# The gate's product of a one-core AdaLN block: tokens standing instead of moving

## The reference

```python
mod = (silu(c) @ wmod)                      # shifts, scales and gates of two halves
h = layernorm(x) * (1 + ca) + sa            # x: 4096 tokens x 256 channels
x = x + ga * linear_attention(h)            # 16 heads of 16, two key/value sets
h = layernorm(x) * (1 + cb) + sb
scores = sigmoid(h @ gate_w + bias)         # gate_w: 256 x 8
top_scores, top_idx = top_k(scores, 2)      # then normalised to weights w
routed = sum over the 2 experts of w * 0.1 * (gelu(h @ up_w + up_b) @ down_w + down_b)
shared = (gelu(h @ sw_up + sb_up) @ sw_down + sb_down) * 0.1
out = shared + routed;  out = out / (max |out| + 1e-6)
x = x + gb * out
```

## Time and profile before

| | |
|---|---|
| median of 3 runs | 975.01 us (974.97 to 976.18) |
| profiled execution, its own time | 978.68 us |
| its span | 976.9 us |
| mean granted clock of TensorE | 0.94 of full |
| TensorE busy in the span | 864.6 us (89%), 5989 products |
| weight loads busy | 793.8 us (81%) |
| VectorE, ScalarE, GpSimd busy | 648.4, 474.5, 415.6 us (66%, 49%, 43%) |

### The profile page before, as it was taken

The page is one execution under the profiler, slowest core; times in us unless marked ns, Lnnn a source line. Parts: engine busy times, 40 slices in busy tenths (PEclk is TensorE's granted clock), DMA queues, the critical chain, the costliest instruction groups (busy, mean ns, idle before and its releaser), DMA issues. The chain is left out here.

```text
span 976.9 us, 21511 instructions
## 1 busy us (share of the span) xinstructions
PE 864.6 (89%) x5989; PEld 793.8 (81%) x5990; DVE 648.4 (66%) x1737; ACT 474.5 (49%) x879; POOL 415.6 (43%) x407
## 2 busy tenths in 40 slices
PE   6899998469999999999873999998999999999982
PEld 5687887458788787787773999998999999999982
DVE  5688775466886786877673676665666666666652
ACT  3665553114544543444442765555556655555530
POOL 3724500211522514414330066655666566666564
PEclk9999999659999998999995999999999999999996
DMA  8120000500210202202248133333333333344442
GB/s 280 56 87 1 1 1 0 172 0 2 89 67 24 90 7 84 89 0 89 80 150 286 52 100 93 92 113 114 87 89 90 90 88 82 78 87 88 100 81 40
DMA packets 64384, 78.58 MB, mean 80 GB/s; under 512 B 23089, under 2 KB 52746, under 8 KB 64176
## 3 DMA queue, kind: packets, MB, share of 16 engines
q0 software_dynamic: 21568, 35.20, 14.5%
q1 hardware_dynamic: 41392, 41.12, 13.5%
q10 hardware_dynamic: 1344, 1.31, 0.4%
HBM read 45.44 MB, written 41.55 MB: 89 GB/s over the span
## 5 line engine op out<-in xcount | busy, mean ns | idle before, releaser
L1668 PE MATMUL psUp<-eT,wup 128*128 128x256 f32 x1632 | 204.8, 286 | 11.4 <-issue 5.7
L1668 PEld LDWEIGHTS psUp<-eT,wup 128*128 128x128 f32 x1632 | 198.5, 192 | 16.5 <-issue 14.3
L1690 PE MATMUL psE<-wdn,gTh 128*128 128x256 f32 x1088 | 199.3, 286 | 0.0
L1690 PEld LDWEIGHTS psE<-wdn,gTh 128*128 128x128 f32 x1088 | 169.8, 193 | 0.0
L1690 PE MATMUL psE<-wdn,gTl 128*128 128x256 f32 x544 | 154.1, 283 | 0.0
L1925 POOL DMA_INDIRECT out<-fin,oidx x68 | 109.3, 1608 | 23.1 <-issue 15.9
L1729 ACT ACTIVATE gu<-psUp,ubias 128x256 f32<-128x256 f32 x272 | 113.4, 468 | 9.9 <-PE psUp L1668 5.0
L1793 DVE TENSOR_TENSOR gTl<-gu,gTh 128x512 fp32r<-128x512 f32 x136 | 93.8, 689 | 32.9 <-ACT gTh L1734 31.4
L1036 PE MATMUL psU<-h2T,su 128*128 128x512 f32 x384 | 109.3, 423 | 4.6 <-ACT gf L1118 4.6
L1748 ACT ACTIVATE ys<-yc,meta 128x256 f32<-128x256 f32 x68 | 30.9, 502 | 165.7 <-DVE yc L1813 165.7
L1906 POOL DMA_INDIRECT gx<-shared_part,meta x68 | 69.4, 1020 | 94.7 <-DMA shared_part<-ys,widx 74.2
(11 more groups left out here) (264 smaller groups left out, 1484.5 us busy)
## 6 DMA issues: line engine op xcount, KB each, us to landing
hin<-expert_in SPq DMA_DIRECT2D x36, 256.0 KB
X<-in_L_attn_x SPq DMA_DIRECT2D x8, 512.0 KB, 7.6
shared_part<-prow SPq DMA_DIRECT2D x8, 512.0 KB, 6.0
out<-X SPq DMA_DIRECT2D x8, 512.0 KB, 4.4
shared_part<-sh SPq DMA_DIRECT2D x7, 512.0 KB, 3.3
raw_up<-in_L_ffn_up_w SPq DMA_DIRECT2D x3, 1024.0 KB, 5.5
raw_dn<-in_L_ffn_down_w SPq DMA_DIRECT2D x3, 1024.0 KB, 9.2
expert_in<-prow SPq DMA_DIRECT2D x8, 272.0 KB, 7.4
```

The costliest lines, as they stand in the source:

```text
L1668: mm = nc.tensor.matmul(psU[:, c, (m % 2) * TR:(m % 2 + 1) * TR], wup[s][:, a, k, m * P:(m + 1) * P], eT[:, u, b, k], start=(n == 0), stop ...
L1690: mm = nc.tensor.matmul(psE[:, u, h * C:(h + 1) * C], (gTh, gTl)[a][:, u, m, h * P:(h + 1) * P], wdn[s][:, b, m], start=(n == 0), stop=(n ...
```

## The change

The gate's product swaps its operands. For each of the four tiles of 128 tokens, the transposed tokens stand (128x128) and 8 weight columns move: 4 x 6 = 24 products instead of 6. The logits come out by token, 128 x 32 in the bank `psZ[0]`, so the copy to `lgT` (`gate_copy`), the four transposes (`turn_gate`), their two semaphores and TensorE's waits for them are left out. `gate_read` takes its input from `psZ`. The gate no longer waits for the last gelu of the stage before, as it does not write `psU`. Since `turn_z(0)` writes the same bank later, it waits for `gate_read` (`gt_ev`). Nothing is changed in the DMAs or on GpSimd and ScalarE.

```diff
--- before.py
+++ after.py
@@ -818,7 +818,6 @@
     rs2 = b2("rs2", [P, 2, 2, TG], F32)
     zT = b2("zT", [P, 2, CK, HALF], F32R)
     z2 = b2("z2", [P, TG, C], F32)
-    lgT = z2[0:E, 0:HALF // C].rearrange("e a c -> e (a c)")
     h2 = b2("h2", [P, 2, TG, ROW], F32)
     h2T = b2("h2T", [P, 2, 2, CK, HALF], F32R)
     gf = b2("gf", [P, 2, HALF], F32)
@@ -904,10 +903,10 @@
 
     names = ("q_pre", "nm_mm", "nm_ev", "rq_ok", "o_mm", "o_ev", "stat2", "self2", "rse2",
              "rstd2", "zo_ok", "tz_mm", "tz_hi", "tz_lo", "xb_ok", "a_mm", "x_ev", "z2_ok", "h2_set", "h2_ok",
-             "th_mm", "th_hi", "th_lo", "gt_row", "gt_cp", "gt_mm", "gt_ev", "gt_sc", "rt_dve", "rt_oh", "rt_mm", "pos_ok",
+             "th_mm", "th_hi", "th_lo", "gt_mm", "gt_ev", "gt_sc", "rt_dve", "rt_oh", "rt_mm", "pos_ok",
              "scat", "u_mm", "u_g", "u_hi", "u_lo", "d_mm", "sh_ev", "sh_st", "x_st", "zero_st")
     (q_pre, nm_mm, nm_ev, rq_ok, o_mm, o_ev, stat2, self2, rse2, rstd2, zo_ok, tz_mm, tz_hi,
-     tz_lo, xb_ok, a_mm, x_ev, z2_ok, h2_set, h2_ok, th_mm, th_hi, th_lo, gt_row, gt_cp, gt_mm, gt_ev, gt_sc, rt_dve, rt_oh,
+     tz_lo, xb_ok, a_mm, x_ev, z2_ok, h2_set, h2_ok, th_mm, th_hi, th_lo, gt_mm, gt_ev, gt_sc, rt_dve, rt_oh,
      rt_mm, pos_ok, scat, u_mm, u_g, u_hi, u_lo, d_mm, sh_ev, sh_st, x_st, zero_st) = [sem(n) for n in names]
 
     def staggered(eng, body):
@@ -929,7 +928,7 @@
         psZ = mem.enter_context(nc.psum_tensor("psZ", [P, 2, HALF], F32))
         psO = mem.enter_context(nc.psum_tensor("psO", [P, HALF], F32))
         psM = mem.enter_context(nc.psum_tensor("psM", [P, HALF], F32))
-        NORM, GATE, RANK, TOTAL = 0, 64, 96, 128
+        NORM, RANK, TOTAL = 0, 96, 128
 
         @block.tensor
         def _(pe):
@@ -960,6 +959,8 @@
 
                 def turn_z(k):
                     pe.wait_ge(zo_ok, TG * g + TG)
+                    if ffn_on and not k:
+                        pe.wait_ge(gt_ev, f + 1)
                     if later(g, 1):
                         pe.wait_ge(th_lo, 2 * g - 1 + k)
                     for t in range(TG):
@@ -991,23 +992,13 @@
                 def gate():
 
                     pe.wait_ge(th_lo, 2 * f + 2)
-                    if later(f, 1):
-                        pe.wait_ge(u_g, MK * f)
-                    n = 0
-                    for k in range(CK):
-                        for a, b in PASSES:
-                            mm = nc.tensor.matmul(psU[0:E, 1], gw[:, b, k], h2T[:, r, a, k],
-                                                  start=(n == 0), stop=(n == 5))
-                            n += 1
-                    mm.then_inc(gt_row, 1)
-
-                def turn_gate():
-                    wait(pe, gt_cp, f + 1)
-                    if att_on:
-                        wait(pe, nm_ev, g + 1)
                     for t in range(TG):
-                        mm = nc.tensor.transpose(psM[:, GATE + t * E:GATE + (t + 1) * E],
-                                                 lgT[:, t * P:(t + 1) * P], ident[0:E, 0:E])
+                        n = 0
+                        for k in range(CK):
+                            for a, b in PASSES:
+                                mm = nc.tensor.matmul(psZ[:, 0, t * E:(t + 1) * E], h2T[:, r, a, k, t * P:(t + 1) * P],
+                                                      gw[:, b, k], start=(n == 0), stop=(n == 5))
+                                n += 1
                     mm.then_inc(gt_mm, 1)
 
                 def rank():
@@ -1064,8 +1055,6 @@
                 chunk(0)
                 if att_on:
                     outs(0)
-                if ffn_on:
-                    turn_gate()
                 chunk(1)
                 if att_on:
                     outs(1)
@@ -1254,14 +1243,9 @@
                     ins.then_inc(rt_dve, 1)
                     wait(dve, rt_dve, ROUTE * f + n[0])
 
-                def gate_copy():
-                    dve.wait_ge(gt_row, f + 1)
-                    dve.wait_ge(h2_ok, TG * f + TG)
-                    nc.vector.tensor_copy(lgT, psU[0:E, 1]).then_inc(gt_cp, 1)
-
                 def gate_read():
                     dve.wait_ge(gt_mm, f + 1)
-                    nc.vector.tensor_tensor(lg[:], psM[:, GATE:GATE + TG * E].rearrange("p (t e) -> p t e", e=E),
+                    nc.vector.tensor_tensor(lg[:], psZ[:, 0, 0:TG * E].rearrange("p (t e) -> p t e", e=E),
                                             gb_row[:].unsqueeze(1).broadcast_to([P, TG, E]), ALU.add
                                             ).then_inc(gt_ev, 1)
 
@@ -1326,8 +1310,6 @@
                 if att_on:
                     norm_read()
                     norm_inverse()
-                if ffn_on:
-                    gate_copy()
                 if att_on:
                     out_read(0)
                 if ffn_on:
```

## The result

The change makes the kernel slower: 1001.4 us median (995.5 to 1002.8, 4 runs) against 975.6 before (975.0 to 978.7, 4 runs), a ratio of 1.023 (95% interval 1.020 to 1.026). The medians are 25.8 us apart; by the ratio it is 22. The forecast was 990 with a range of 977 to 997: right direction, too small by 11 us, outside the range. The profiled executions, 978.7 and 1002.1 us, are 23.4 apart where the forecast had 15, so some 3 of the 11 us are the spread between executions and 8 are the forecast's.

What follows compares the result with a forecast made beforehand. Each stage was taken as bound by gate start to `up(2)`, 8.83 us, lengthened by thin products and lost clock. Short spells +12.1, long +17.7, middle +15 on 975.0 gave 990.0 us, range 977 to 997.

Steps and rivals of the forecast that it cites:

- The chain and the place: Gate start to `up(2)`: gate, `up(0)`, `outs(0)`, attention read, logits read, sigmoid, gelu(0); 8.83 us before, its delay delays the stage.
- The pace of a small product: New gate's 24 products take the norms' pace: 0.116 us each at full clock (2.78 us), 0.214 at half (5.13).
- The full-clock sum of 9.30 us per stage: Gate start to `up(2)` without any clock effect: 9.30 us against 8.83, +0.5.
- The direction of the clock: TensorE's clock was expected to fall to half in nearly every stage, in or right after the gate.
- The place of the fall: The clock falls on average half-way through the gate: 12 products at full clock, 12 at half.
- Rows 4 (long): Stage at half clock through norms, gate and all of `up(0)`; the long spell in seven later stages gives +17.7 us.
- rows 6 (short): Clock falls near 367.7 and is back at 371.1, 3.4 us; the short spell sums to +12.1 us.
- So a stretch of thin products is enough to lose the clock: Norms plus gate, thin for 3.3 to 3.9 us before, 4.7 to 5.3 after, lose the clock without a real pause.
- The clock as before: Rival: the clock falls only where it fell before; +4.4 us, 979.4 us, chance 0.11.
- the swallowed loss: Rival: gapless gate products count as work, no fall is left; +0.7 us, 975.7 us, chance 0.08.
- the faster one: Rival: standing loads run ahead, gate product under 0.096 us, `outs(0)` ends earlier; about -7, 968 us, chance 0.06.

Runs made afterwards that it cites:

- the best version: Kernel before, wide gate kept, its logits in the other bank, copy, turns and logits read moved later, sigmoid behind gelu(1): 966.3 us, 0.987.
- the kernel with filler: Kernel after with 12 dense products of 512 columns added per stage, result unread, ahead of the gate's wait and between its thin products: 1013.9 us, 1.038.

## Why the prediction was wrong in size

**Right.** The chain and the place: all of the loss lies between the gate's start and `up(2)`, and the rest of each stage passes it on unchanged. The pace of a small product, from the row of the norms, 0.116 us at full and 0.214 at half clock. The last gate, all thin products at full clock, took 2.70 us, 0.113 each; the first, all at half, 5.12, 0.213 each. The two kinds of instruction in after:

```profile
L999 PEld LDWEIGHTS psZ<-gw,h2T x192: 186/216/338, 213.8 to 503.9; 128*128 128x128 f32 x192
L999 PE MATMUL psZ<-gw,h2T x192: 252/281/356, 213.8 to 504.0; 128*128 128x8 f32 x192
```

Their own durations (0.19 to 0.34 for a load, 0.25 to 0.36 for a product) say little; the pace is in the starts. The 81 ns of the Trainium skill (TensorE: Matmul & The Clock Gate, Back-to-back issue gap) for such a pair were not seen in this kernel with f32 loads. The full-clock sum of 9.30 us per stage was met by the stages that kept it: 9.44 with 128 columns, 9.56 with 256 of which 0.2 is the longer stream. The direction of the clock was right: each of the eight stages had half clock. The place of the fall was right on average too: in the stages 2 to 7 the clock fell 6, 16, 12, 4, 19 and 16 products into the gate, 12 in the mean, which is the half-way that the forecast took.

**Wrong.** The step that failed is the length of the spell: "Rows 4 (long) and rows 6 (short) both exist, so I take the middle". Short gave +12.1 us, long +17.7; measured +22.7 between gate and `up(2)`. Between gate and `up(2)`, each of the stages 2 to 7 had 6.8 us of half clock or more, none a single spell of 3.4. The stage at 254.91 was forecast at 10.9 or 11.7 us and took 12.6: there the clock fell after 6 of the 24 products and not after 12, so the gate took 4.57 us where I had 3.96, and `up(0)` 2.70 for 2.56. In the five stages behind it `outs(0)` was at half clock as well, 1.56 us to the start of `up(1)` where 0.8 to 0.9 is usual, and I had put it at full. Leaving out the fifth stage, that is 0.3 to 1.0 us per stage beyond the long case. The fifth, which had two spells before and for which I had +0.1 (short) or +0.9 (long), got 10.2 us of half clock and +2.7. The first gate cost +3.3 in place of +2.6, again by `outs(0)` and `up(1)` at half. The last was +1.3 as forecast, but that was luck: the forecast had the spell inside the gate, and in the trace the whole gate ran at full clock (2.70 us for 1.40), the clock fell 0.7 us into `up(0)`, and gate end to `up(2)` took 4.4 us as before, as the turns (0.34) and the wait of 0.95 were gone.

Behind it stands a reason that was wrong: "So a stretch of thin products is enough to lose the clock" was right, but I counted the old gate into that stretch, "whose products use 8 columns of the array". The two kernels with twelve added products speak against it: behind 6 products with 8 standing and 512 moving columns the twelve kept the clock in six of seven later stages of the trace, ahead of them they lost it in all seven. That rests on one trace of each, and four of ten executions of the first kernel were as slow as the second. By that reading the thin stretch of before was the norms alone, 1.85 us, and the change made it 4.6, two and a half times as long and not 40% longer. In the trace the rest of it then ran at half clock, which stretched it (the gate took 3.2 to 4.8 us in stages 2 to 7), and the clock was back only in `outs(0)` or `up(1)`, behind 2.7 us of `up(0)`. That the spell is 6.8 us and not 3.4 because the block is so long is argued, not shown: the same block behind `outs(0)` still had one spell of 6.8 among shorter ones.

**The rivals.** The clock as before (979.4) and the swallowed loss (975.7) are out by the clock column; the faster one (968) by the pace. Its "about -7" does not come out of the terms given for it (-4.8, the lost falls of 3.7 and 1.2 for the first gate are -9.7), which changes nothing here. The rule of the Trainium skill quoted there (TensorE: Matmul & The Clock Gate, Why this matters for your kernels), to keep TensorE continuously busy, is not enough in this trace: the thin gate follows the norms without idle time at 254.91 and the clock is gone before it ends.

**How the loss divides.** With 256 moving columns the same number of products and loads gave 987.1: about 14 of the 22 to 26 us go with the clock, and the other 8 to 12 are the added work (1.3 us per stage, less 0.3 for the turns), with what the remaining spells add. Half clock between norms and `up(2)` grew by 30.5 us; as work at half clock takes twice its time, that is an estimated 15 us, which fits. It is not a strict split, as that kernel has 0.2 us more work per stage and its own chance of spells.

## What to carry to other kernels

Swapping the operands so that the big one stands turns 6 long streams into 24 weight loads with almost nothing behind them; the price is not only the loads' pace (24 x 0.113 against 6 x 0.235 us) but the clock of everything around. If such thin products are needed, try dealing them out between dense ones instead of running them as a block, above all not next to another thin block: here this alone was worth 23 us with the same products, once the sigmoid was late. And before a result's way is shortened, ask who waits for it: the sigmoid two places later in ScalarE's order gave 8 us, most of what the best version gained.

## What was not expected of the hardware

- The same twelve products cost 7 us behind the old gate's products and 15 us ahead of them (medians; 8 and 15 by the ratios), though four of ten executions of the first order were as slow as the second.
- 128 moving columns per load of 128 standing ones (24 at 0.114 us) did not hold the clock; 256 (0.122 us) mostly did.
- Once down, the clock can stay down under a full queue of mixed work: in the kernel with filler for 10.2 us, with no idle time of TensorE between the gate's start and `up(0)`.
- Which exact mix lets the clock fall, and why the same stage of the same kernel keeps it in one case and not in the next, was not settled. Executions of one kernel lie about 1% apart (973.7 to 983.1 us for before, 980.8 to 993.3 for the twelve behind the gate); whether that is the reason was not shown.
